# h1 split in rows and transposed by DMA in a two-layer graph attention kernel

## The chip, the cores and the metric

One core of one Trainium2 chip runs the whole program in one launch. The metric is the device time of an execution in microseconds; lower is better. Times of the profile count from the start of the profiled execution's span.

## The reference, cut to what matters

```python
x = _layernorm(x + gcn(x, W))                       # 1250 nodes, 768 features
h = gat_conv(x, W1, heads=4, out_ch=256)            # layer one: attention over the edges
h = relu(layer_norm(h, g1, be1))
h1 = h + (x @ Wr1 + br1)                            # 1250 x 1024
h = gat_conv(h1, W2, heads=1, out_ch=768)           # layer two; begins with h1 @ W2
h = layer_norm(h, g2, be2) + (h1 @ Wr2 + br2)
out = _layernorm(x + h)
```

In `gat_conv` each node sums the projected rows of its neighbours with softmax weights. Layer two needs two products of the same matrix, `h1 @ W2` and `h1 @ Wr2`.

## The kernel before, in words

The 1250 nodes are padded to 1280 and cut into T = 10 tiles of 128. Edges are counted into a dense 1280 x 1280 matrix, so that each attention is a dense matrix product. Every engine has its own hand-written list of instructions, in which it runs strictly in order; semaphores are the only ties between the lists. All DMAs that matter here are issued by SP (SyncE), one list as well: a wait in it holds up everything behind it.

Layer one's attention runs in 2 halves of the destination nodes (5 tiles each), each half in 4 heads, each head in 10 source tiles: 80 steps. In a step DVE makes the larger of two sums (L1576), ACT takes its exponential (L1163), DVE multiplies it by the edge counts (L1591), and PE multiplies the weights with the projected rows for 5 destination tiles (`attend1`, L972; float32, so each product shows as two instructions in the trace). DVE may be up to five steps ahead of PE (five weight buffers). `ATT_BANKS` (L99) gives each of the five sums of a head its PSUM bank: in the first half the heads walk over eight banks, in the second over six, since banks 6 and 7 hold `p_h`. When a head is done ACT evicts its five banks (`evict`), DVE makes the reciprocals (`sums`, L1564), ACT scales (`scale`).

A finished tile t of the attention, `att[t]` (128 nodes x 1024 features, float32), is normalized by DVE (`norm_start`, `norm_end`: L1406 to L1610), which also adds layer one's residual that SP loaded into `r_ld[t % 2]` (`residual`, L517). That is h1. Layer two's products need h1 with features on the partitions and in two float16 halves, high and low, since a product of halves is summed as high x high, high x low and low x high. Before the change a tile goes this way: PE transposes it by eight float32 128 x 128 transposes into `p_h`, two PSUM banks (`h1_transposes`, L960); ACT casts `p_h` to the high half (`h1_high`, L1139, in the helper L1060); DVE subtracts that from `p_h` for the low half (`h1_low`, L1615). There is one `p_h`, so the next tile's transposes wait for the low half of the one before.

Tiles 0 and 1 go this way inside the second half of the attention: DVE normalizes them at steps 9 and 18 (`NORM_AT`), PE transposes them after steps 11 and 20 (`TR_AT`), ACT and DVE split them at 15 and 26 (`H1_AT`). Tiles 2 to 9 follow behind the attention, where PE runs the list `LAYER2`: transposes `tr`, products with W2 `x` (48 matmuls each, `product2`, L945) and two products with Wr2 `r`; the other eight `r` come after it (L1019). Each product writes two adjoining banks, by turns one of two pairs (`p_x`), and waits in `slot_free` until the product two before it has been evicted. ACT and DVE meanwhile split W2 and Wr2 into halves (`weights(3)`, `weights(4)`, L1066 and L1257), whose rows SP loads two at a time, evict the products (`xl2_high`, `xl2_low`), and DVE normalizes the remaining tiles. On SP the loads of weights, residuals and of layer one's shift rows (`rows`) stand in one order, L519 to L552; `residual(t)` waits until tile t - 2 is normalized (L516), because the buffer is shared.

After the last `x` product, PE lays out a row of layer two's scores (`rows_of`, L986), DVE takes maxima, and the second attention (L1053) follows.

Earlier in the program SP already transposes something by DMA: ten transposes of 128 x 1280 two-byte elements (L462), in SBUF on both sides.

Of the kernel before, what the change touches and what calls it, by code (L numbers as in the profile page):

```python
# [74 lines left out]
C1 = 5  # L75
# [6 lines left out]
TR_AT = {11: 0, 20: 1}  # L82
H1_AT = {15: 0, 26: 1}
# [4 lines left out]
LAYER2 = ["tr2", "x0", "tr3", "x1", "x2", "tr4", "x3", "tr5", "x4", "tr6", "r0", "x5", "tr7", "r1", "tr8", "x6", "tr9", "x7", "x8", "x9"]  # L88
# [10 lines left out]
ATT_BANKS = [[(ch * C1 + j) % 8 for j in range(C1)] for ch in range(H)]  # L99
ATT_BANKS += [[(4 + ch * C1 + j) % 6 for j in range(C1)] for ch in range(H)]  # L100
# [8 lines left out]
def banks_read(ch, n):  # L109

    return ch * 2 * C1 + n
# [11 lines left out]
def gnn_program(nc, x, src, dst, W0, b0, W1, a_src1, a_dst1, b1, g1, be1, Wr1, br1,  # L123
# [7 lines left out]
    with ExitStack() as ctx:  # L131
# [152 lines left out]
        r_ld = [at(115 * KB, [HC], f32), at(119 * KB, [HC], f32)]  # L284
        h1t_hi = [at((b + 2 * j) * KB, [KH, P], f16) for b in (146, 95) for j in range(C1)]
# [56 lines left out]
        p_h = psum[:, 512 * 6:512 * 8]  # L342
# [12 lines left out]
        def everywhere(row):  # L355
# [13 lines left out]
            ln_var ln_rstd h1_ok h1_tr h1t_hi_ok h1t_lo_ok r_in0 r_in1   # L369
# [52 lines left out]
        PRODUCTS = [(step[0], int(step[-1])) for step in LAYER2 if step[0] != "t"] + [("r", t) for t in range(AHEAD_R, T)]  # L422
        X2_SLOT = [PRODUCTS.index(("x", t)) % 2 for t in range(T)]
        R2_SLOT = [PRODUCTS.index(("r", t)) % 2 for t in range(T)]
# [4 lines left out]
        def _(sp):  # L429
# [82 lines left out]

            def residual(t):

                if t >= 2:
                    sp.wait_ge(S["h1_ok"], t - 1)  # L516
                sp.dma_start(r_ld[t % 2], r1_d[t]).then_inc(S[f"r_in{t % 2}"], 16)  # L517
# [18 lines left out]
            rows(1, 2)  # L536
            weights(3, [2])
            rows(1, 3)
            residual(2)
            residual(3)  # L540
            weights(3, range(3, KH))
            sp.wait_ge(S["larger_ok"], 2 * H * T)
            weights(4, [0, 1])
            residual(4)
            weights(4, [2, 3])
            residual(5)
            residual(6)
# [145 lines left out]
        def _(pe):  # L693
# [260 lines left out]
            def h1_transposes(t):  # L954

                pe.wait_ge(S["h1_ok"], t + 1)
                if t:
                    pe.wait_ge(S["h1t_lo_ok"], t)
                for k in range(KH):
                    last = pe.transpose(p_h[:, k * P:(k + 1) * P], att[t][:, k * P:(k + 1) * P], ident)  # L960
                last.then_inc(S["h1_tr"], 1)
# [16 lines left out]
            for n in range(H * T):  # L978
                attend1(H * T + n)
                if n in TR_AT:  # L980
                    h1_transposes(TR_AT[n])
# [7 lines left out]
            def r2_first(t):  # L989

                product2(p_x[R2_SLOT[t]], t, W_PARTS[4], range(KH // 2))

            def r2_second(t):

                product2(p_x[R2_SLOT[t]], t, W_PARTS[4], range(KH // 2, KH)).then_inc(S["r2_done"], 1)

            def slot_free(i):

                if i < 2:
                    pe.wait_ge(S["att_read"], banks_read(2 * H - 1, C1 - 2 * (1 - i)))  # L1000
                else:
                    what, t = PRODUCTS[i - 2]
                    pe.wait_ge(S["xl2_lo_ok" if what == "x" else "r2_sb"], t + 1)
# [3 lines left out]
            for step in LAYER2:  # L1007
                t = int(step[-1])
                if step[:-1] == "tr":
                    h1_transposes(t)  # L1010
                else:
                    slot_free(PRODUCTS.index((step[0], t)))
                    if step[0] == "x":
                        xl2_tile(t)
                    else:
                        pe.wait_ge(S["w_lo"], W_FIRST[4] + KH)
                        r2_first(t)
                        r2_second(t)
# [39 lines left out]
        def _(act):  # L1058
# [74 lines left out]
            def xl2_high(t):  # L1133
                act.wait_ge(S["xl2_done"], t + 1)
                cast(xl2_hi[:, t, 0:D], p_x[X2_SLOT[t]][:, 0:D], S["xl2_hi_ok"], 1 / WSCALE)
# [34 lines left out]
            for n in range(H * T):  # L1170
                if n in W2_AT:
                    k = W2_AT.index(n)
                    act.wait_ge(S["p_free"], (H + 1 + (k > 2) + (k == KH - 1)) * T)
                    weights(3, [k])
                    if k == KH - 1:
                        act.wait_ge(S["w2a_split"], 2)
                        for m, part in enumerate((w2a_hi, w2a_lo)):
                            cast(w2_rows[:, :, m, D:XS], part[:, 0:KH - 1, :], S["w2x_ok"])
                            cast(w2_last[:, m, D:XS], part[:, KH - 1, :], S["w2x_ok"])
                if n in H1_AT:  # L1180
                    h1_high(H1_AT[n])
                exps(H * T + n)
# [3 lines left out]
            weights(4, [0, 1])  # L1186
            xl2_high(0)
            h1_high(3)
            weights(4, [2, 3])
            xl2_high(1)  # L1190
            weights(4, [4, 5])
            xl2_high(2)
            h1_high(4)
            weights(4, [6, 7])
            xl2_high(3)
            h1_high(5)
            xl2_high(4)
            h1_high(6)
            xl2_high(5)
            h1_high(7)  # L1200
# [47 lines left out]
        def _(dve):  # L1248
# [303 lines left out]
            def xl2_low(t):  # L1552

                p = p_x[X2_SLOT[t]]
# [72 lines left out]
            for n in range(H * T):  # L1627
                if n - 1 in W2_AT:
                    weights(3, [W2_AT.index(n - 1)])
                if n in H1_AT:  # L1630
                    h1_low(H1_AT[n])
# [12 lines left out]
            def r2_evict(t):  # L1644
# [4 lines left out]
                dve.scalar_tensor_tensor(to, p_x[R2_SLOT[t]][:, 0:D], 1 / WSCALE, xb, ALU.mult, ALU.add).then_inc(S["r2_sb"], 1)  # L1649
# [15 lines left out]
            norm_end(5)  # L1665
            weights(4, [4, 5])
            xl2_low(2)
            h1_low(4)
            norm_start(6)
            weights(4, [6, 7])  # L1670
            norm_end(6)
            xl2_low(3)
            h1_low(5)
# [7 lines left out]
            h1_low(6)  # L1681
            dve.wait_ge(S["dve"], steps_done())
            xb_sum(0)
            norm_start(8)
# [3 lines left out]
            h1_low(7)  # L1688
# [4 lines left out]
            h1_low(8)  # L1693
            xl2_low(6)
            h1_low(9)
# [150 lines left out]
```

## Time and profile before

| what | us |
|---|---|
| median of 3 runs | 851.09 |
| lowest and highest of them | 849.22, 853.28 |
| profiled execution, its own time | 851.03 |
| profiled execution, its span | 849.2 |

The span runs from the first to the last recorded instruction; 1.83 us of the execution lie around it. The profiled execution stands 0.06 us below the median. In the trace a row of a timeline has start, length, engine, line, operation, operands and count; in brackets is the idle time of the engine before it and what ended that. A merged row's length runs from its first start to its last end. The granted clock of TensorE is a fraction of 2.4 GHz.

### The profile page before, as it was taken

How to read it: one execution, taken by the hardware profiler on the slowest of the kernel's cores; microseconds unless marked ns; L12 is line 12 of the kernel's file. 1: busy time of each engine (PE TensorE's matmuls, PEld its weight loads, DVE VectorE, ACT ScalarE, POOL GpSimd, SP SyncE). 2: the span in 40 equal slices, each digit the busy share in tenths (PEclk: the TensorE clock that was granted, in tenths of full speed). 3: DMA queues.
4: the chain of work that ended last, by engine and by line, in shares of the span. 5: the costliest groups of instructions: out<-in, count | busy, mean ns of one | idle time of the engine just before them, and what ended most of it. 6: DMA issues, size and time to landing. Idle time of an engine off the chain costs nothing.

```text
span 849.2 us, 13556 instructions
## 1 busy us (share of the span) xinstructions
PE 818.0 (96%) x4922; PEld 526.0 (62%) x4922; DVE 670.3 (79%) x1181; ACT 270.3 (32%) x510; POOL 58.8 (7%) x77
## 2 busy tenths in 40 slices
PE   5999999999999999998999998999999999999995
PEld 4566666456454444436888887886666666655553
DVE  7998885778567849998888879969873196996686
ACT  3444444300111101014545545644301107760000
POOL 2000002000203000000000000002110000001111
PEclk9999999999999999999999999999999999999998
DMA  8000003114912474226111203213213242212232
GB/s 307 3 2 2 1 2 107 63 53 170 176 42 69 137 246 166 85 89 215 64 52 58 90 7 118 74 64 124 88 63 94 94 150 76 79 57 75 75 112 71
DMA packets 37709, 76.82 MB, mean 90 GB/s; under 512 B 15877, under 2 KB 16877, under 8 KB 37519
## 3 DMA queue, kind: packets, MB, share of 16 engines
q1 hardware_dynamic: 36382, 70.89, 25.3%
q0 software_dynamic: 1264, 5.11, 2.0%
q8 instruction: 38, 0.62, 0.3%
q14 instruction: 25, 0.20, 0.1%
HBM read 52.40 MB, written 20.31 MB: 86 GB/s over the span
## 4 chain that ended last, share of the span: by engine, by line
PE 80%; DVE 10%; DMA 3%; issue 3%; SPq 2%; DVEq 1%; ACT 1%; POOL 0%; POOLq 0%
PE psum L945 18%; PE psum L972 18%; PE psum L1053 12%; PE psum L868 8%; PE psum L747 8%; DVE arena L1445 6%; PE psum L759 6%; PE psum L811 4%; SPq L462 2%; PE psum L804 1%; PE psum L960 1%; PE psum L986 1%; DMA uv_scratch<-arena 1%; DMA arena<-as_scratch 1%; PE psum L720 1%
## 5 line engine op out<-in xcount | busy, mean ns | idle before, releaser
L972 PE MATMUL psum<-arena 128*128 128x257 f32 x800 | 175.4, 381 | 4.9 <-DVE arena L1591 3.8
L1060 ACT ACTIVATE arena<-psum 128x160 f16<-128x160 f32 (+6 forms) x188 | 93.3, 527 | 250.3 <-PE psum L747 73.9
L972 PEld LDWEIGHTS psum<-arena 128*128 128x128 f32 x800 | 151.2, 190 | 28.6 <-issue 2.7
L747 PE MATMUL psum<-arena 128*128 128x512 f16 x720 | 158.4, 379 | 2.3 <-DVE arena L1417 2.1
L945 PE MATMUL psum<-arena 128*128 128x512 f16 x960 | 158.5, 326 | 0.2 <-ACT arena L1060 0.2
L945 PEld LDWEIGHTS psum<-arena 128*128 128x128 f16 x960 | 93.5, 97 | 62.3 <-ACT arena L1060 0.5
L747 PEld LDWEIGHTS psum<-arena 128*128 128x128 f16 x720 | 69.5, 98 | 87.8 <-issue 7.0
L1053 PE MATMUL psum<-arena 128*128 128x512 f16 (+2 forms) x600 | 98.4, 325 | 0.0
L1445 DVE CUSTOM_DVE_ANT_0 arena<-arena 128x1280 bf16<-128x1280 bf16 x50 | 71.0, 1486 | 15.7 <-DMA arena<-as_scratch 9.8
L1053 PEld LDWEIGHTS psum<-arena 128*128 128x128 f16 x600 | 58.3, 97 | 39.8
L1163 ACT ACTIVATE arena<-arena 128x640 f32<-128x640 f32 x80 | 64.6, 835 | 52.8 <-DVE arena L1576 52.6
L1591 DVE SCALAR_TENSOR_TENSOR arena<-arena 128x640 f32<-128x640 f32 x80 | 65.2, 817 | 15.4 <-ACT arena L1163 9.6
L1060 ACT ACTIVATE arena<-arena 128x768 f16<-128x768 f32 (+4 forms) x58 | 45.7, 805 | 88.2 <-DMA arena<-in_L_gnn_Wr_dram 43.2
L1576 DVE SCALAR_TENSOR_TENSOR arena<-arena 128x640 f32<-128x640 f32 x80 | 70.0, 876 | 2.2 <-DMA arena<-uv_scratch 2.2
L868 PE MATMUL psum<-arena 128*128 128x512 f16 (+1 forms) x400 | 66.7, 326 | 2.7 <-DVE arena L1400 1.9
L759 PE MATMUL psum<-arena 128*128 128x512 f16 x360 | 68.5, 325 | 0.0
L868 PEld LDWEIGHTS psum<-arena 128*128 x400 | 38.3, 98 | 30.8 <-issue 6.2
L1359 DVE TENSOR_TENSOR arena<-arena 128x960 f16<-128x960 int16 x80 | 51.9, 649 | 0.0
L811 PE MATMUL psum<-arena 128*128 128x160 f16 x480 | 48.3, 235 | 1.6 <-DVE arena L1359 1.5
L1358 DVE TENSOR_TENSOR arena<-arena 128x768 f16<-128x768 int16 x80 | 44.2, 552 | 6.1 <-PE psum L811 2.4
L1455 DVE CUSTOM_DVE_ANT_0 arena<-psum,arena 128x256 bf16<-128x256 f32 x80 | 28.4, 420 | 19.8 <-PE psum L747 19.8
L759 PEld LDWEIGHTS psum<-arena 128*128 128x128 f16 x360 | 33.2, 97 | 15.5
(167 smaller groups left out, 695.5 us busy)
## 6 DMA issues: line engine op xcount, KB each, us to landing
arena<-in_L_gnn_W_dram SPq DMA_DIRECT2D x22, 384.0 KB, 3.6
r_scratch<-arena SPq DMA_DIRECT2D x10, 512.0 KB, 2.8
arena<-uv_scratch SPq DMA_DIRECT2D x16, 320.0 KB, 4.2
arena<-r_scratch SPq DMA_DIRECT2D x10, 512.0 KB, 3.7
x_scratch<-arena SPq DMA_DIRECT2D x10, 384.0 KB, 4.7
arena<-x_scratch SPq DMA_DIRECT2D x10, 384.0 KB, 3.5
r_scratch<-arena SPq DMA_DIRECT2D x10, 384.0 KB, 2.6
arena<-r_scratch SPq DMA_DIRECT2D x10, 384.0 KB, 4.0
```

What stands on the lines that cost most here:

```text
L747: ins = pe.matmul(o[:, a:b], part[:, k, ds(t * P, P)], w[:, k, a:b], start=(not begun and k == 0 and n == 0 and m == 0), stop=(k == kn - 1 ...
L759: last = pe.matmul(p_out[t % 2][:, a:b], part[:, k, t * P:(t + 1) * P], w[:, k, a:b], start=(k == 0 and name == "hh"), stop=(k == KD - 1 a ...
L811: last = pe.matmul(o, ring_lo[slot][:, i // 2, :, i % 2], ring_key[slot][:, i // 2, :, i % 2], start=False, stop=False, skip_group_check=True)
L868: ins = pe.matmul(p_out[par][:, a:b], counts, part[:, k, a:b], start=(not low and k == 0 and n == 0), stop=(not low and k == T - 1 and n = ...
L945: ins = pe.matmul(o[:, a:b], part[:, k, :], w[k][:, a:b], start=(k == 0 and n == 0 and m == 0), stop=(k == KH - 1 and n == 1))
L972: last = pe.matmul(p_att[:, ATT_BANKS[ch][j], 0:HID + 1], pf[n % PSLOTS][:, j * P:(j + 1) * P], xl[ch % H][:, k, 0:HID + 1], start=(k == 0 ...
L1053: last = pe.matmul(p_att2[c % 2][:, j, a:b], p[n][:, t % C1 * P:(t % C1 + 1) * P], xl2[:, k, a:b], start=(k == 0 and m == 0), stop=(k == T ...
L1060: act.activation(out_, in_, ACT.Copy, scale=scale).then_inc(signal, 1)
L1163: act.activation(ee[s], ee[s], ACT.Exp, bias=as_s[:, ch % H, k:k + 1]).then_inc(S["ex_ok"], 1)
L1445: dve.tensor_tensor_reduce(out=out_, in0=mask, in1=row, scale=1.0, scalar=NEG_BIG, op0=ALU.add, op1=ALU.max, accum_out=mx[:, col, t:t + 1] ...
L1576: dve.scalar_tensor_tensor(ee[s], u_row, asd[:, ch % H, k:k + 1], v_row, ALU.add, ALU.max).then_inc(S["larger_ok"], 1)
L1591: dve.scalar_tensor_tensor(pf[n % PSLOTS], ee[s], 1.0, CT[:, k, ds(ch // H * W1C, W1C)], ALU.min, ALU.mult).then_inc(S["pf_ok"], 1)
```

## The change

h1 is now split into halves before it is transposed. ACT casts `att[t]` as it lies, nodes on partitions, into a high half, DVE subtracts it for the low half, and SP sends each half through a DMA transpose of 128 x 1024 float16 into the same `h1t_hi[t]` and `h1t_lo[t]` as before. The halves (`h1_rows`) lie in the memory of the residual buffer `r_ld[t % 2]`, so `residual(t)` now waits until both transposes of tile t - 2 have landed. PE's transposes are gone, and with them `p_h`: the second half's attention banks walk over all eight, and layer two's products take turns over four bank pairs. The lists of SP, ACT and DVE are re-ordered to fit.

```diff
-TR_AT = {11: 0, 20: 1}
-H1_AT = {15: 0, 26: 1}
+HIGH_AT = {11: 0, 20: 1}
+LOW_AT = {12: 0, 22: 1}
-LAYER2 = ["tr2", "x0", "tr3", "x1", "x2", "tr4", "x3", "tr5", "x4", "tr6", "r0", "x5", "tr7", "r1", "tr8", "x6", "tr9", "x7", "x8", "x9"]
+LAYER2 = ["x0", "x1", "x2", "x3", "x4", "x5", "r0", "x6", "r1", "x7", "x8", "x9"]
-ATT_BANKS = [[(ch * C1 + j) % 8 for j in range(C1)] for ch in range(H)]
-ATT_BANKS += [[(4 + ch * C1 + j) % 6 for j in range(C1)] for ch in range(H)]
+ATT_BANKS = [[(ch * C1 + j) % 8 for j in range(C1)] for ch in range(2 * H)]
+        h1_rows = [[at((115 + 4 * i + 2 * m) * KB, [HC], f16) for i in range(2)] for m in range(2)]
-        p_h = psum[:, 512 * 6:512 * 8]
+        p_x2 = [psum[:, 1024 * i:1024 * (i + 1)] for i in range(4)]
+        SLOTS = [i % 4 for i in range(len(LAYER2))] + [1 + t % 2 for t in range(AHEAD_R, T)]
...
+            def h1_across(t):
+
+                for m, (made, to) in enumerate((("h1_hi_ok", h1t_hi[t]), ("h1_lo_ok", h1t_lo[t]))):
+                    sp.wait_ge(S[made], t + 1)
+                    sp.dma_start_transpose(to, h1_rows[m][t % 2]).then_inc(S[f"h1t_in{t % 2}"], 16)
+
             def residual(t):
 
                 if t >= 2:
-                    sp.wait_ge(S["h1_ok"], t - 1)
+                    sp.wait_ge(S[f"h1t_in{t % 2}"], 32 * (t // 2))
...
             rows(1, 2)
+            h1_across(0)
             weights(3, [2])
+            residual(2)
             rows(1, 3)
-            residual(2)
+            h1_across(1)
+            weights(3, [3])
             residual(3)
-            weights(3, range(3, KH))
+            weights(3, range(4, KH))
             sp.wait_ge(S["larger_ok"], 2 * H * T)
             weights(4, [0, 1])
+            h1_across(2)
             residual(4)
             weights(4, [2, 3])
+            h1_across(3)
             residual(5)
+            weights(4, [4, 5])
+            h1_across(4)
             residual(6)
-            weights(4, [4, 5])
+            weights(4, [6, 7])
+            h1_across(5)
             residual(7)
-            weights(4, [6, 7])
+            h1_across(6)
             residual(8)
-            residual(9)
...
+            h1_across(7)
+            residual(9)
             r2_store(0)
...
-            sp.wait_ge(S["h1_tr"], T)
+            h1_across(8)
+            h1_across(9)
...
             def xl2_tile(t):
 
-                pe.wait_ge(S["h1t_lo_ok"], t + 1)
-                product2(p_x[X2_SLOT[t]], t, W2_WIDE, range(KH), XS).then_inc(S["xl2_done"], 1)
+                pe.wait_ge(S[f"h1t_in{t % 2}"], 32 * (t // 2 + 1))
+                product2(p_x2[X2_SLOT[t]], t, W2_WIDE, range(KH), XS).then_inc(S["xl2_done"], 1)
...
                 if t == AHEAD_R:
                     pe.wait_ge(S["as2_ok"], 1)
+                    pe.wait_ge(S["xl2_lo_ok"], T)
+                    pe.wait_ge(S["r2_sb"], AHEAD_R)
...
             def h1_high(t):
-                act.wait_ge(S["h1_tr"], t + 1)
-                cast(h1t_hi[t], p_h.rearrange("p (k n) -> p k n", k=KH), S["h1t_hi_ok"])
+                act.wait_ge(S["h1_ok"], t + 1)
+                cast(h1_rows[0][t % 2], att[t], S["h1_hi_ok"])
...
             def h1_low(t):
 
-                dve.wait_ge(S["h1t_hi_ok"], t + 1)
-                dve.tensor_tensor(h1t_lo[t], p_h.rearrange("p (k n) -> p k n", k=KH), h1t_hi[t], ALU.subtract).then_inc(S["h1t_lo_ok"], 1)
+                dve.wait_ge(S["h1_hi_ok"], t + 1)
+                dve.tensor_tensor(h1_rows[1][t % 2], att[t], h1_rows[0][t % 2], ALU.subtract).then_inc(S["h1_lo_ok"], 1)
...
             sums(2 * H - 1)
+            h1_low(2)
             norm_start(3)
-            h1_low(2)
             norm_end(3)
             weights(4, [0, 1])
+            h1_low(3)
             norm_start(4)
             xl2_low(0)
-            h1_low(3)
             norm_end(4)
             weights(4, [2, 3])
+            h1_low(4)
             norm_start(5)
             xl2_low(1)
+            weights(4, [4, 5])
             norm_end(5)
-            weights(4, [4, 5])
+            h1_low(5)
```

The rest of DVE's list and ACT's list change in the same manner: each `h1_high(t)` and `h1_low(t)` now stands as soon as tile t is normalized.

## Rows read from the trace of the kernel before

**Rows 1.** The profile page, part 1: engine, busy us (share), instructions.

```profile
PE 818.0 (96%) x4922; PEld 526.0 (62%) x4922; DVE 670.3 (79%) x1181; ACT 270.3 (32%) x510; POOL 58.8 (7%) x77
```

**Rows 2.** Stretches: length, busy PE, PEld, DVE, ACT, POOL; clock, DMA share, GB/s.

```profile
500.00:521.00 21.00, 20.27 (x96) 17.37 (x96) 16.50 (x23) 10.85 (x20) 1.52 (x1) 1.00 0.23 76
...
580.00:600.00 20.00, 20.00 (x126) 12.16 (x125) 19.79 (x29) 7.10 (x9) 3.03 (x2) 1.00 0.56 183
```

**Rows 3.** Timeline of PE, attention's second half: start, us, line, [idle before <-releaser].

```profile
500.16 4.17 PE L972 MATMUL psum<-arena 128*128 128x257 f32 x18 [0.17 <-ACT arena L1060]
504.17 1.04 PE L960 MATMUL psum<-arena 128*128 128x128 f32 x8
...
521.99 2.87 PE L972 MATMUL psum<-arena 128*128 128x257 f32 x12 [1.55 <-DVE arena L1591]
525.57 2.00 PE L972 MATMUL psum<-arena 128*128 128x257 f32 x8 [0.72 <-ACT arena L1060]
...
548.56 21.51 PE L972 MATMUL psum<-arena 128*128 128x257 f32 x98 [0.17 <-ACT arena L1060]
569.90 1.04 PE L960 MATMUL psum<-arena 128*128 128x128 f32 x8
571.16 8.05 PE L945 MATMUL psum<-arena 128*128 128x512 f16 x48 [0.22 <-ACT arena L1060]
```

**Rows 4.** Line L960, TensorE's transposes: ns least/median/most.

```profile
L960 PE MATMUL psum<-arena x80: 272/272/273, 504.2 to 647.9; 128*128 128x128 f32 x80
```

**Rows 5.** Timeline of PE, layer two: the last transposition, then products.

```profile
647.13 1.04 PE L960 MATMUL psum<-arena 128*128 128x128 f32 x8
648.00 27.68 PE L945 MATMUL psum<-arena 128*128 128x512 f16 x168
```

**Rows 6.** Timelines of DVE, then ACT, around the attention's first transposition.

```profile
506.30 1.23 DVE L1615 TENSOR_TENSOR arena<-psum,arena 128x1024 f16<-128x1024 f32 x1 [3.44 <-ACT arena L1060]
...
505.24 1.02 ACT L1060 ACTIVATE arena<-psum 128x1024 f16<-128x1024 f32 x1 [3.32 <-PE psum L960]
```

**Rows 7.** Line L462, the ten DMA transposes: issue, then issue to landing.

```profile
L462 SPq DMA_TRANSPOSE arena<-arena x10: 1336/1606/3169, 216.1 to 232.8; - x10
...
DMA to landing us min/median/max: 3.6/4.4/6.2
```

**Rows 8.** Timeline of SP: the ten transposes, then weights beside the attention.

```profile
216.09 18.33 SPq L462 DMA_TRANSPOSE arena<-arena  x10
...
513.67 0.33 SPq L446 DMA_DIRECT2D arena<-in_L_gnn_W_dram  x1
...
525.94 23.91 SPq L446 DMA_DIRECT2D arena<-in_L_gnn_W_dram  x5
```

**Rows 9.** Lines L1615 and L1610 on DVE: ns least/median/most.

```profile
L1615 DVE TENSOR_TENSOR arena<-psum,arena x10: 1210/1217/1226, 506.3 to 649.3; 128x1024 f16<-128x1024 f32 x10
...
L1610 DVE SCALAR_TENSOR_TENSOR arena<-arena x10: 1224/1225/1226, 493.2 to 638.2; 128x1024 f32<-128x1024 f32 x10
```

**Rows 10.** ACT's groups by line and shape, 480 to 680 us.

```profile
L1060 ACT ACTIVATE arena<-arena 128x768 f16<-128x768 f32 x16 | 13.4, 844 | 9.1 <-DMA arena<-in_L_gnn_Wr_dram 8.8
...
L1060 ACT ACTIVATE arena<-psum 128x1024 f16<-128x1024 f32 x10 | 10.3, 1028 | 11.3 <-PE psum L960 11.0
```

**Rows 11.** Timeline of ACT, from 569 to 600 us.

```profile
570.18 2.40 ACT L1060 ACTIVATE arena<-psum 128x256 f32<-128x256 f32 x6
...
592.86 1.77 ACT L1060 ACTIVATE arena<-arena 128x768 f16<-128x768 f32 x2 [4.05 <-DMA arena<-in_L_gnn_Wr_dram]
```

**Rows 12.** Timeline of the SP queue beside layer two.

```profile
588.48 1.20 SPq L446 DMA_DIRECT2D arena<-in_L_gnn_Wr_dram  x2
```

**Rows 13.** Timeline of DVE: where two tiles' statistics start in layer two.

```profile
580.12 1.28 DVE L1406 BATCH_NORM_STATS2 arena<-arena 128x6 f32<-128x512 f32 x2
...
589.19 1.28 DVE L1406 BATCH_NORM_STATS2 arena<-arena 128x6 f32<-128x512 f32 x2
```

More of the change, by code:

```diff
@@ L368, in gnn_program @@
             uv_free uv_ok uv_tr uv_rows uv_dram uvr0 uvr1 ex_ok larger_ok pf_ok p_free rsum_ok att_read
-            ln_var ln_rstd h1_ok h1_tr h1t_hi_ok h1t_lo_ok r_in0 r_in1
+            ln_var ln_rstd h1_ok h1_hi_ok h1_lo_ok h1t_in0 h1t_in1 r_in0 r_in1
             w2a_in0 w2a_in1 w2a_ok w2a_split w2x_ok as2_ok as2_rows asr2
@@ L420, in gnn_program @@
                        [[w2[k][:, m, 0:D] for k in range(KH)] for m in range(2)], [wr2_hi, wr2_lo]]
-        PRODUCTS = [(step[0], int(step[-1])) for step in LAYER2 if step[0] != "t"] + [("r", t) for t in range(AHEAD_R, T)]
-        X2_SLOT = [PRODUCTS.index(("x", t)) % 2 for t in range(T)]
-        R2_SLOT = [PRODUCTS.index(("r", t)) % 2 for t in range(T)]
+        PRODUCTS = [(step[0], int(step[-1])) for step in LAYER2] + [("r", t) for t in range(AHEAD_R, T)]
+        SLOTS = [i % 4 for i in range(len(LAYER2))] + [1 + t % 2 for t in range(AHEAD_R, T)]
+        X2_SLOT = [SLOTS[PRODUCTS.index(("x", t))] for t in range(T)]
+        R2_SLOT = [SLOTS[PRODUCTS.index(("r", t))] for t in range(T)]
         UV2_AT = (5, 6)
@@ L949, in xl2_tile @@
             def xl2_tile(t):
-                pe.wait_ge(S["h1t_lo_ok"], t + 1)
-                product2(p_x[X2_SLOT[t]], t, W2_WIDE, range(KH), XS).then_inc(S["xl2_done"], 1)
[L954 to L961, printed above, removed]
+                pe.wait_ge(S[f"h1t_in{t % 2}"], 32 * (t // 2 + 1))
+                product2(p_x2[X2_SLOT[t]], t, W2_WIDE, range(KH), XS).then_inc(S["xl2_done"], 1)
             def attend1(n):
@@ L979, in _ @@
                 attend1(H * T + n)
-                if n in TR_AT:
-                    h1_transposes(TR_AT[n])
             def rows_of(column, tiles, o):
@@ L989, in r2_first @@
             def r2_first(t):
-                product2(p_x[R2_SLOT[t]], t, W_PARTS[4], range(KH // 2))
+                product2(p_x2[R2_SLOT[t]], t, W_PARTS[4], range(KH // 2))
             def r2_second(t):
-                product2(p_x[R2_SLOT[t]], t, W_PARTS[4], range(KH // 2, KH)).then_inc(S["r2_done"], 1)
+                product2(p_x2[R2_SLOT[t]], t, W_PARTS[4], range(KH // 2, KH)).then_inc(S["r2_done"], 1)
             def slot_free(i):
-                if i < 2:
-                    pe.wait_ge(S["att_read"], banks_read(2 * H - 1, C1 - 2 * (1 - i)))
-                else:
-                    what, t = PRODUCTS[i - 2]
-                    pe.wait_ge(S["xl2_lo_ok" if what == "x" else "r2_sb"], t + 1)
+                before = [n for n in range(i) if SLOTS[n] == SLOTS[i]]
+                if before:
+                    what, t = PRODUCTS[before[-1]]
+                    pe.wait_ge(S["xl2_lo_ok" if what == "x" else "r2_sb"], t + 1)
+                elif SLOTS[i] == 0:
+                    pe.wait_ge(S["att_read"], banks_read(2 * H - 2, C1 - 1))
+                else:
+                    pe.wait_ge(S["att_read"], banks_read(2 * H - 1, 2 * SLOTS[i] - 1))
             pe.wait_ge(S["w_lo"], W_FIRST[4])
@@ L1008, in _ @@
                 t = int(step[-1])
-                if step[:-1] == "tr":
-                    h1_transposes(t)
-                else:
[L1012 to L1018, printed above, removed]
+                slot_free(PRODUCTS.index((step[0], t)))
+                if step[0] == "x":
+                    xl2_tile(t)
+                else:
+                    pe.wait_ge(S["w_lo"], W_FIRST[4] + KH)
+                    r2_first(t)
+                    r2_second(t)
             for t in range(AHEAD_R, T):
@@ L1134, in xl2_high @@
                 act.wait_ge(S["xl2_done"], t + 1)
-                cast(xl2_hi[:, t, 0:D], p_x[X2_SLOT[t]][:, 0:D], S["xl2_hi_ok"], 1 / WSCALE)
+                cast(xl2_hi[:, t, 0:D], p_x2[X2_SLOT[t]][:, 0:D], S["xl2_hi_ok"], 1 / WSCALE)
             def h1_high(t):
-                act.wait_ge(S["h1_tr"], t + 1)
-                cast(h1t_hi[t], p_h.rearrange("p (k n) -> p k n", k=KH), S["h1t_hi_ok"])
+                act.wait_ge(S["h1_ok"], t + 1)
+                cast(h1_rows[0][t % 2], att[t], S["h1_hi_ok"])
             def evict(ch):
@@ L1179, in _ @@
                             cast(w2_last[:, m, D:XS], part[:, KH - 1, :], S["w2x_ok"])
-                if n in H1_AT:
-                    h1_high(H1_AT[n])
+                if n in HIGH_AT:
+                    h1_high(HIGH_AT[n])
                 exps(H * T + n)
@@ L1186, in _ @@
             weights(4, [0, 1])
+            h1_high(3)
             xl2_high(0)
-            h1_high(3)
             weights(4, [2, 3])
+            h1_high(4)
             xl2_high(1)
             weights(4, [4, 5])
+            h1_high(5)
             xl2_high(2)
-            h1_high(4)
             weights(4, [6, 7])
             xl2_high(3)
-            h1_high(5)
+            h1_high(6)
             xl2_high(4)
-            h1_high(6)
+            h1_high(7)
             xl2_high(5)
-            h1_high(7)
             h1_high(8)
@@ L1552, in xl2_low @@
             def xl2_low(t):
-                p = p_x[X2_SLOT[t]]
+                p = p_x2[X2_SLOT[t]]
                 dve.wait_ge(S["xl2_hi_ok"], t + 1)
@@ L1629, in _ @@
                     weights(3, [W2_AT.index(n - 1)])
-                if n in H1_AT:
-                    h1_low(H1_AT[n])
+                if n in LOW_AT:
+                    h1_low(LOW_AT[n])
                 if n in NORM_AT:
@@ L1648, in r2_evict @@
                 to, xb = (r_early, r_early) if t < AHEAD_R else (r2_st[t % 2], xb_ld[t % 2])
-                dve.scalar_tensor_tensor(to, p_x[R2_SLOT[t]][:, 0:D], 1 / WSCALE, xb, ALU.mult, ALU.add).then_inc(S["r2_sb"], 1)
+                dve.scalar_tensor_tensor(to, p_x2[R2_SLOT[t]][:, 0:D], 1 / WSCALE, xb, ALU.mult, ALU.add).then_inc(S["r2_sb"], 1)
             norm_start(2)
@@ L1653, in _ @@
             sums(2 * H - 1)
+            h1_low(2)
             norm_start(3)
-            h1_low(2)
             norm_end(3)
             weights(4, [0, 1])
+            h1_low(3)
             norm_start(4)
             xl2_low(0)
-            h1_low(3)
             norm_end(4)
             weights(4, [2, 3])
+            h1_low(4)
             norm_start(5)
             xl2_low(1)
+            weights(4, [4, 5])
             norm_end(5)
-            weights(4, [4, 5])
+            h1_low(5)
+            norm_start(6)
             xl2_low(2)
-            h1_low(4)
-            norm_start(6)
             weights(4, [6, 7])
             norm_end(6)
+            h1_low(6)
             xl2_low(3)
-            h1_low(5)
             dve.wait_ge(S["par_br2"], 16)
@@ L1680, in _ @@
             norm_end(7)
-            h1_low(6)
             dve.wait_ge(S["dve"], steps_done())
             xb_sum(0)
+            h1_low(7)
             norm_start(8)
@@ L1687, in _ @@
             xl2_low(5)
-            h1_low(7)
+            h1_low(8)
             norm_start(9)
@@ L1692, in _ @@
             r2_evict(1)
-            h1_low(8)
+            h1_low(9)
             xl2_low(6)
-            h1_low(9)
             xl2_low(7)
```

## The prediction

> **What bounds the kernel now.** I read the page first: PE is busy for 818.0 us of 849.2 [rows 1], so it matters what keeps PE busy and where it pauses. Next, the busy times by stretch: beside the attention PE works 20.27 of 21.0 us, and in layer two 20.00 of 20.0, while DVE there works 19.79 and the DMA engines 0.56 of their time for 183 GB/s [rows 2]. The granted clock is 1.00, the 2.4 GHz level, in both. So around the change PE is the bound, and DVE has almost nothing left in layer two. PE's timeline then shows the few pauses: 0.17, 1.55, 0.72 and 0.17 us in the attention's second half, 0.22 ahead of the first product [rows 3]. Everything that PE is spared here shortens the kernel, as long as nothing else comes late.
>
> **The transposes that go.** Eighty of them [rows 4], ten tiles of eight. One tile takes PE 0.87 us, from 647.13 to the next product at 648.00 [rows 5]. In the attention two stand in the row of work (504.17 [rows 3] is the first): 2 x 0.87 = 1.74 us. The third stands between the attention and the first product; from 569.90 to 571.16 are 1.26 us, the 0.22 us pause in it [rows 3]. The other seven: 6.09 us. Together **9.09 us**, all on PE's path.
>
> **The pauses in the attention.** The 1.55 us pause ends with a weight from DVE [rows 3]. DVE was late because it had itself stood 3.44 us before its low half of tile 0, waiting for ACT's cast, and ACT had stood 3.32 us for PE's transposes [rows 6]: ACT and DVE run ahead of PE and were made to wait for it. With the cast taken from `att[t]`, that circle is gone; the cast needs only DVE's own normalization. DVE gets back 3.44 us, PE needs its weights at most 1.55 + 0.87 + 0.17 = 2.59 us sooner, so 0.85 us are left and I count the pause as gone. The pauses of 0.17, 0.72 and 0.17 us are waits for ACT's evictions: with six banks, four of a head's five have been used by the head just before; with eight, only two, and PE comes to them after three other sums. I count them as gone: 0.17 + 1.55 + 0.72 + 0.17 = **2.61 us**.
>
> **The four bank pairs** are worth nothing by themselves: no product in layer two waits for its pair, and 168 matmuls from 648.00 run without a bracket in 27.68 us, or 7.9 us for a product's 48 [rows 5]. The new waits before the score row (all `xl2_low`, two `r2` evictions) stand behind work that DVE has ahead of `as2_ok`, which PE awaits there already. I take zero; the cover is DVE's order. The loads for the `r2` evictions, which stood behind PE's last transposes on SP, now stand behind the last DMA transposes; x8 and x9 cover them.
>
> **What is added: twenty DMA transposes on SP.** The row that comes nearest is the kernel's own ten, 128 x 1280 of the same two-byte kind: SP takes 1.34, 1.61, 3.17 us for one (least, median, most), and it lands 3.6, 4.4, 6.2 us after its issue [rows 7]. All ten go out in 18.33 us [rows 8]. Ours have eight blocks in place of ten. Those ten ran back to back, ours run between loads of residuals and weights; so I take the median, unscaled, as the likely cost, and keep both ends. The Trainium skill speaks against this part of the change (VectorE: DVE Perf Modes, The three transpose paths and Rules for kernel authors): a 128 x 128 transpose costs 390 ns on TensorE and 1309 ns through the DMA crossbar, and TensorE is the one to use where PSUM will do. A hundred blocks at that price would be 131 us, an estimate by that page; the trace disagrees with its 18.33 us [rows 8].
>
> The casts and subtractions only change their source. The subtraction from PSUM took 1.22 us, a DVE instruction on float32 from SBUF of the same size 1.225 us [rows 9]. ACT's cast from PSUM took 1.03 us; 768 elements from SBUF took 0.84, so 1024 between 1.03 and 1.13 us [rows 10]. Zero for both. ACT's cast of tile 0 now waits at step 11 for DVE, which has h1 ready at 493.2 + 1.2 = 494.4 [rows 9], eleven microseconds ahead of the old cast [rows 6]; behind it stand exponentials that DVE needs, but the cast was on ACT's list before too, so it adds nothing to the list, only shifts one cast four steps forward.
>
> **What is queued behind the new waits on SP.** In the attention `h1_across(0)` stands ahead of W2's third piece, which in the trace went out only at 513.67, and `h1_across(1)` ahead of the next, followed by pieces spaced over 23.91 us [rows 8]; the low halves of both tiles are due well before (steps 12 and 22), so the pieces lose at most the issue time, 2 x 1.61 us, on a queue that is waiting anyway. Zero, between 0 and 3 us of a DVE wait that PE has five weights against.
>
> In layer two it is tighter. PE would begin x0 at 571.16 - 1.74 - 1.26 - 2.61 = 565.55 us, and product x_t (t up to 5) is due at 565.55 + 7.87 t; x2 at 581.3, x5 at 604.9. ACT's cast of tile 2 stands behind the last eviction: together they end at 570.18 + 2.40 = 572.58, which is 2.68 us after the attention [rows 3, 11]; now 565.55 + 2.68 = 568.2. There `h1_across(2)` starts. SP's loop from tile to tile is two issues I, the landing D (residual t + 2 waits for it, and everything stands behind that), and some 1.5 us for a residual and two weights, 1.20 of it for the weights [rows 12]: L = 2I + D + 1.5. Tile 5 lands at 568.2 + 3L + 2I + D = 566.7 + 4L, so x5 is late by **4L - 38.2 us**. With the medians L = 3.22 + 4.4 + 1.5 = 9.1: early by 1.8. With the least values L = 7.8, early by 7. With the most L = 14.0, late by 18. A queue of loads ahead of the transposes can lengthen D: weights issued at 588.48 behind a residual released ACT at 592.86, 4.4 us on [rows 11, 12], no more than the transposes' own median. DVE has its own pace: from one tile's statistics to the next 580.12 to 589.19, 9.07 us [rows 13]. From the low half of tile 2 at 568.2 + 1.2 = 569.4, three such and one wait for ACT's cast (1.0) give 597.6 for the low half of tile 5, landed 1.6 + 4.4 later at 603.6; due 604.9. The margin is 1.3 us. After x5 stands r0, which needs no new tile, and after x6 stands r1, so later tiles have more. I put **0.7 us** of delay at x5, between 0 and 18.
>
> **The sum**, against the profiled execution's own 851.03 us (0.06 below the median of the runs, which is nothing): 851.03 - 9.09 - 2.61 + 0.7 = 840.03, so **840.0 us**.
>
> **The rivals.** First, layer two is paced by tiles, not by PE: L of 10 to 11.3, or a DVE pace of 10 us in place of 9.07. Then x5, and x3 and x4 before it, are late by 2 to 7 us: 841.3 to 846.3. For it: DVE is full there and the margin is 1.3 us. Against: both medians say otherwise. Second, DVE remains the bound in the attention, because 0.85 us of margin is little, and the 2.61 us stay: 842.6. Third, slower than before: the transposes, mixed with loads, cost what the dearest of the ten did. L = 14.0 and x5 starts 18 us late: 851.03 - 11.7 + 18 = 857.3. It decides from L = 13.5 on, where 4L - 38.2 exceeds 11.7 + 4.3. For it: the row's 3.17 and 6.2 us exist; against: each is one of ten, and issue and landing would have to be at their worst together. The Trainium skill's page named above (VectorE: DVE Perf Modes) points this way and further: sixteen blocks at 1309 ns are 20.9 us a tile, an estimate by that page, by which L would be 26.8 and the time 908; the ten transposes of the trace bear it out in nothing, and I give it no more than this rival's chance. Last, nothing changes: what PE is spared is waited for in full, x5 late by 11.7 us, L = 12.5: 851.
>
> **How the numbers follow.** The forecast (no delay to 2 us at x5) has 0.66, the first rival 0.16, the second 0.06, the third 0.06, no change 0.06. A measurement of this kernel can tell about 0.5% from no change, 4.3 us; faster means below 846.8. Forecast, second rival and nearly all of the first make 0.86, less a little for what I have not seen: 0.85. Same 0.08, slower 0.07. Range: low end 11.7 us off and the spread of runs below their median, 1.9: 851.03 - 11.7 - 1.9 = 837.4; high end within the first rival, 846.0. That leaves out about 0.19.
>
> **What would show it.** Right: no line of transposes on PE, no bracket over 0.2 us in the attention's second half, x0 at about 565.5, the score row at some 663 to 665, a DMA transpose of 1.2 to 1.7 us on SP. First rival: brackets on PE before x3 to x5 that end with a DMA. Second: a bracket near 520 that ends with DVE. Third: issues of 3 us and landings of 6. Wrong altogether if the transposes hold up the loads so that DVE or ACT wait for weights inside the attention.

## The result and the profile after

The changed kernel takes **836.85 us** (median of 4 runs, 835.29 to 837.94) against 850.74 us for the kernel before (4 runs): a ratio of 0.9832, 95% interval 0.9803 to 0.9862. The prediction said 840.0 us and 837.4 to 846.0: the direction was right, the gain of 13.9 us is larger than forecast, and the time lies 0.55 us below the low end of the range. The profiled execution takes 836.33 us, its span 834.5. One of the ten executions of the run that splits later, below, took 1220.27 us at a mean granted clock of 0.654 and is left out of its median.

The page, part 1, of the changed kernel, then its PE timeline from the attention to the second attention; these rows answer to [rows 1, 3, 5].

```profile
PE 807.4 (97%) x4842; PEld 517.7 (62%) x4842; DVE 670.2 (80%) x1181; ACT 269.2 (32%) x509; POOL 58.8 (7%) x77
```

```profile
389.13 173.65 PE L980 MATMUL psum<-arena 128*128 128x257 f32 x800 [0.98 <-DVE arena L1599]
562.62 98.39 PE L962 MATMUL psum<-arena 128*128 128x512 f16 x600
660.85 2.40 PE L992 MATMUL psum<-arena 128*128 128x128 f32 x20
...
726.04 9.23 PE L1061 MATMUL psum<-arena 128*128 128x512 f16 x55
```

PE is busy for 807.4 us, 10.6 less, and from the attention's first product on what is left runs without a bracket: 800 attention products in one row, right behind it layer two's 600 matmuls in one row up to the score row at 660.85. No line of transposes is left on PE. The stages, before and after, from their first rows:

| stage | before, us | after, us | gain, us |
|---|---|---|---|
| ahead of the attention | 390.67 | 389.13 | 1.54 |
| attention, with two of the ten transpositions | 179.23 | 173.49 | 5.74 |
| from the attention's end to the second attention | 170.82 | 163.42 | 7.40 |
| second attention, end, and what lies around the span | 110.31 | 110.29 | 0.02 |

The gain in the two stages that were changed is 5.74 + 7.40 = **13.14 us**. The busy times by stretch answer to [rows 2]:

```profile
500.00:521.00 21.00, 21.00 (x99) 18.38 (x98) 20.63 (x29) 13.01 (x24) 1.52 (x1) 1.00 0.29 88
580.00:600.00 20.00, 20.00 (x124) 11.85 (x122) 18.67 (x26) 7.58 (x9) 3.03 (x2) 1.00 0.81 184
```

PE works all the time in each stretch; DVE works 20.63 of 21.0 us in the first and 18.67 of 20.0 in the second; the share of the DMA engines in the second rose from 0.56 to 0.81 while they moved 184 GB/s in place of 183, the transposes' bytes included. The new transposes, line L518, answer to [rows 7]:

```profile
L518 SPq DMA_TRANSPOSE arena<-arena x20: 1232/1254/2742, 494.0 to 635.6; - x20
...
DMA to landing us min/median/max: 3.0/3.5/5.7
```

SP takes 1.25 us for one in the median, between the least and the median of the ten taken in proportion (0.8 x 1.34 = 1.07 us, 0.8 x 1.61 = 1.29 us), and it lands in 3.5 us.

### The profile page after: what moved, and what is told of

The parts are those of the page before. It is cut to its first block, busy times and chain, and to the rows that moved or that the text cites. A ratio compares the mean times of both kernels' runs of the same rounds, so it can differ in the third digit from the quotient of the medians.

```text
span 834.5 us, 13407 instructions
## 1 busy us (share of the span) xinstructions
PE 807.4 (97%) x4842; PEld 517.7 (62%) x4842; DVE 670.2 (80%) x1181; ACT 269.2 (32%) x509; POOL 58.8 (7%) x77
## 4 chain that ended last, share of the span: by engine, by line
PE 83%; DVE 9%; DMA 3%; SPq 2%; issue 2%; DVEq 1%; ACT 1%; POOL 0%; POOLq 0%
PE psum L980 21%; PE psum L962 19%; PE psum L1061 12%; PE psum L885 8%; PE psum L764 8%; DVE arena L1453 6%; PE psum L776 6%; PE psum L828 5%; SPq L463 2%; PE psum L821 1%; PE psum L737 1%; PE psum L992 1%; DMA arena<-as_scratch 1%; PE psum L839 1%; DMA arena<-uv_scratch 1%
## 5 line engine op out<-in xcount | busy, mean ns | idle before, releaser
L980 PE MATMUL psum<-arena 128*128 128x257 f32 x800 | 173.6, 380 | 1.0 <-DVE arena L1599 1.0
L1068 ACT ACTIVATE arena<-psum 128x160 f16<-128x160 f32 (+5 forms) x178 | 83.1, 498 | 206.7 <-PE psum L764 73.7
L962 PEld LDWEIGHTS psum<-arena 128*128 128x128 f16 x960 | 93.6, 97 | 62.8
L764 PEld LDWEIGHTS psum<-arena 128*128 128x128 f16 x720 | 69.5, 98 | 88.4 <-issue 7.6
L1068 ACT ACTIVATE arena<-arena 128x1024 f16<-128x1024 f32 (+3 forms) x68 | 56.2, 842 | 135.5 <-DVE arena L1618 47.7
L1061 PEld LDWEIGHTS psum<-arena 128*128 128x128 f16 x600 | 58.3, 97 | 39.8
L1103 ACT ACTIVATE arena<-psum 128x160 uint16<-128x160 f32 x80 | 24.4, 305 | 57.6 <-PE psum L776 36.7
```

The costliest lines, as they stand in the source:

```text
L764: ins = pe.matmul(o[:, a:b], part[:, k, ds(t * P, P)], w[:, k, a:b], start=(not begun and k == 0 and n == 0 and m == 0), stop=(k == kn - 1 ...
L962: ins = pe.matmul(o[:, a:b], part[:, k, :], w[k][:, a:b], start=(k == 0 and n == 0 and m == 0), stop=(k == KH - 1 and n == 1))
L980: last = pe.matmul(p_att[:, ATT_BANKS[ch][j], 0:HID + 1], pf[n % PSLOTS][:, j * P:(j + 1) * P], xl[ch % H][:, k, 0:HID + 1], start=(k == 0 ...
L1061: last = pe.matmul(p_att2[c % 2][:, j, a:b], p[n][:, t % C1 * P:(t % C1 + 1) * P], xl2[:, k, a:b], start=(k == 0 and m == 0), stop=(k == T ...
L1068: act.activation(out_, in_, ACT.Copy, scale=scale).then_inc(signal, 1)
```

## The experiments

**Six attention banks again.** The changed kernel; layer two's pairs in another order, so that x0 finds a free one.

```diff
-ATT_BANKS = [[(ch * C1 + j) % 8 for j in range(C1)] for ch in range(2 * H)]
+ATT_BANKS = [[(ch * C1 + j) % 8 for j in range(C1)] for ch in range(H)]
+ATT_BANKS += [[(4 + ch * C1 + j) % 6 for j in range(C1)] for ch in range(H)]
...
-        SLOTS = [i % 4 for i in range(len(LAYER2))] + ...
+        SLOTS = [(3, 1, 2, 0)[i % 4] for i in range(len(LAYER2))] + ...
...
```

> The changed kernel with the second half's attention sums on six banks again; everything else stays, the transposes on DMA too (layer two's products start on other pairs so that x0 need not wait). Before, the attention lost 4.0 us to pauses (179.23 us from its first product to its end, less 1.74 us of transposes, less 800 products at the 0.2169 us that one takes in the changed kernel). Theory: some 2.2 us of these are waits for ACT's evictions that six banks bring by themselves, the rest (1.55 us and the end of a product that the bracket does not count) is DVE. Then the attention takes 175.5 to 176 us here, against 173.5 in the changed kernel, and the time is about 839. Rival: ACT was late only because it had stood for PE's transposes; then six banks cost under 0.5 us and the time stays at 837.

Measured: 838.59 us, ratio 0.9862 (0.9827 to 0.9896). Its PE timeline:

```profile
388.89 109.33 PE L981 MATMUL psum<-arena 128*128 128x257 f32 x502 [1.29 <-DVE arena L1599]
498.39 21.94 PE L981 MATMUL psum<-arena 128*128 128x257 f32 x100 [0.17 <-ACT arena L1068]
520.51 21.94 PE L981 MATMUL psum<-arena 128*128 128x257 f32 x100 [0.17 <-ACT arena L1068]
542.62 21.51 PE L981 MATMUL psum<-arena 128*128 128x257 f32 x98 [0.17 <-ACT arena L1068]
563.97 36.25 PE L963 MATMUL psum<-arena 128*128 128x512 f16 x220
```

The attention takes 563.97 - 388.89 = 175.08 us, **1.59 us more** than the 173.49 us of the changed kernel. The theory holds; its size, 2.0 to 2.5 us, was too high. What readers should see: the brackets add up to 0.51 us, a third of what was lost.

**The kernel before, splitting later.**

```diff
-H1_AT = {15: 0, 26: 1}
+H1_AT = {18: 0, 27: 1}
```

> The kernel before with one line changed: ACT and DVE split tiles 0 and 1 at steps 18 and 27 of the attention's second half in place of 15 and 26; PE's transposes stay where they were. Theory: ACT stood 3.32 us for PE's transposes and DVE 3.44 us for ACT, and that made PE's 1.55 us pause near 522; asked three steps later, ACT finds the transposes done, both waits go, and PE's pause with them (1.55 us and the 0.16 us by which a product's length exceeds its share of the row): the attention takes 177.3 us or less from its first product to its end against 179.23, and the time is 848.5 to 849. Rival: DVE is late there by its own work (two normalizations in ten steps); then the bracket on PE that ends with DVE stays above 1 us and the time stays at 850.

Measured: 846.89 us (median of nine), ratio 0.9973 (0.9956 to 0.9990). The timelines of PE, then of ACT and of DVE at the first split:

```profile
388.72 109.33 PE L972 MATMUL psum<-arena 128*128 128x257 f32 x502 [1.25 <-DVE arena L1591]
498.22 4.17 PE L972 MATMUL psum<-arena 128*128 128x257 f32 x18 [0.17 <-ACT arena L1060]
...
503.10 17.94 PE L972 MATMUL psum<-arena 128*128 128x257 f32 x82
521.21 2.00 PE L972 MATMUL psum<-arena 128*128 128x257 f32 x8 [0.17 <-ACT arena L1060]
...
565.54 1.04 PE L960 MATMUL psum<-arena 128*128 128x128 f32 x8
```

```profile
503.30 1.02 ACT L1060 ACTIVATE arena<-psum 128x1024 f16<-128x1024 f32 x1 [0.45 <-PE psum L960]
```

```profile
507.08 1.22 DVE L1615 TENSOR_TENSOR arena<-psum,arena 128x1024 f16<-128x1024 f32 x1
```

ACT's cast waits 0.45 us where it waited 3.32, DVE's subtraction has no bracket where it had 3.44 [rows 6], and PE's bracket that ended with DVE is gone. So is most of the one of 0.72 us that ended with ACT: 0.17 is left. The attention takes 565.54 - 388.72 = 176.82 us, **2.41 us less** than before, with all of PE's transposes in place. The circle was the cause, and DVE's own work was not too much. What this attention still loses is 176.82 - 1.74 - 173.49 = 1.59 us, the same as with the six banks alone. So the two explain 2.41 + 1.59 = 4.00 us, all that the attention lost to pauses.

**PE's transposes put back as dead work.**

```diff
                 pe.wait_ge(S[f"h1t_in{t % 2}"], 32 * (t // 2 + 1))
+                for k in range(KH):
+                    pe.transpose(p_x2[X2_SLOT[t]][:, k * P:(k + 1) * P], ident, ident)
                 product2(p_x2[X2_SLOT[t]], t, W2_WIDE, range(KH), XS).then_inc(S["xl2_done"], 1)
```

> The changed kernel with eight float32 transposes of the identity put on PE before each of the ten x products; their results are overwritten and nothing waits for them. PE's work is then that of before, the waits are those of the changed kernel. Theory: PE's time is the path in all of layer two, so 10 x 0.87 = 8.7 us come back: 545.5 or so for 836.85 + 8.7 = 845.5. Rival: part of PE's spared time is waited for elsewhere (DVE's pace of 9 to 10 us a tile), then under 6 us come back, below 843.

(845.5 is meant where the text has 545.5.) Measured: 844.26 us, ratio 0.9924 (0.9898 to 0.9950). Its PE timeline:

```profile
564.90 1.04 PE L970 MATMUL psum<-arena 128*128 128x128 f32 x8
565.78 8.03 PE L962 MATMUL psum<-arena 128*128 128x512 f16 x48
...
609.51 15.84 PE L962 MATMUL psum<-arena 128*128 128x512 f16 x96
...
671.87 2.40 PE L994 MATMUL psum<-arena 128*128 128x128 f32 x20
```

From the attention's end at 564.90 to the score row at 671.87 are 106.97 us against 660.85 - 562.62 = 98.23: **8.74 us**, ten times the 0.87 us of one transposition [rows 5] within 0.04. PE's time is the path here, and nothing gives any of it back.

**Two bank pairs in layer two.**

```diff
-        SLOTS = [i % 4 for i in range(len(LAYER2))] + ...
+        SLOTS = [1 + i % 2 for i in range(len(LAYER2))] + ...
```

> The changed kernel with layer two's products on two bank pairs by turns in place of four (banks 2 to 5, as before the change). The prediction's step: the four pairs are worth nothing by themselves; then 0.6 us are lost before x0, which waits for the first eviction, and nothing later: about 837.5. Rival: in the changed order of DVE's list an eviction of a product comes two to five microseconds after the product two places on is due (the low half of x2 ends at 598.4, x4 is due at 594.1), so PE pauses before x3, x4, x6 and x7, in all 8 to 13 us: 845 to 850, most of the gain gone.

Measured: **853.61 us**, ratio 1.0044 (1.0026 to 1.0062): slower than the kernel before. PE's timeline, then two of the low halves on DVE:

```profile
564.02 23.78 PE L962 MATMUL psum<-arena 128*128 128x512 f16 x144 [0.74 <-ACT arena L1068]
588.64 8.05 PE L962 MATMUL psum<-arena 128*128 128x512 f16 x48 [0.83 <-DVE arena L1566]
598.93 23.72 PE L962 MATMUL psum<-arena 128*128 128x512 f16 x144 [2.25 <-DVE arena L1566]
627.09 18.39 PE L962 MATMUL psum<-arena 128*128 128x512 f16 x96 [4.44 <-DVE arena L1566]
648.60 29.36 PE L962 MATMUL psum<-arena 128*128 128x512 f16 x168 [3.12 <-DVE arena L1566]
677.80 2.40 PE L992 MATMUL psum<-arena 128*128 128x128 f32 x20
```

```profile
597.92 0.95 DVE L1566 SCALAR_TENSOR_TENSOR arena<-psum,arena 128x768 f16<-128x768 f32 x1
...
626.08 0.95 DVE L1566 SCALAR_TENSOR_TENSOR arena<-psum,arena 128x768 f16<-128x768 f32 x1
```

PE starts x4 at 598.93, when DVE's low half of x2 ends (597.92 + 0.95), and x6 at 627.09, when that of x5 ends (626.08 + 0.95). The rival holds in its mechanism, and its size, 845 to 850, was too small: the brackets add up to 11.38 us, but the stage, from the attention's end (it starts at 389.64, and 389.64 + 173.49 = 563.13) to 677.80, takes 16.44 us more than 98.23. Some 0.8 is the length of a product in front of each bracket. The rest is in the matmuls: 96 of them from 627.09 take 18.39 us, where e3's 96 took 15.84. The busy times by stretch say why:

```profile
598.90:622.60 23.70, 23.67 (x144) 13.94 (x144) 18.10 (x24) 3.74 (x4) 3.03 (x2) 1.00 0.51 109
627.00:633.00 6.00, 5.91 (x21) 2.90 (x22) 5.60 (x9) 0.19 (x1) 1.51 (x1) 0.56 0.73 150
633.00:639.00 6.00, 6.00 (x38) 3.53 (x37) 1.79 (x2) 1.28 (x2) 1.13 (x2) 1.00 0.41 124
648.60:654.00 5.40, 5.40 (x23) 2.82 (x24) 0.00 (x0) 0.00 (x0) 0.00 (x0) 0.68 0.94 241
```

The third figure from the end of a row, behind POOL's, is the granted clock: 1.00 between the pauses of 2.25 and 4.44 us, a mean of 0.56 for the 6 us after the one of 4.44 us, then 1.00 again, and 0.68 for 5.4 us after the one of 3.12.

**Three bank pairs.**

```diff
-        SLOTS = [i % 4 for i in range(len(LAYER2))] + ...
+        SLOTS = [i % 3 for i in range(len(LAYER2))] + ...
```

> The changed kernel with layer two's products on three bank pairs by turns. With two pairs PE paused 11.4 us for DVE's low halves of the products two places back (the longest, 4.44 us, before x6). Theory: a third pair gives each eviction one product more, 7.9 us, which is longer than the longest pause, so none is left, and the time is that of the changed kernel, 837. Rival: DVE's lateness grows as PE no longer waits for it (9 to 10 us a tile against PE's 7.9), then pauses of 1 to 4 us are left before x5 or x7 and the time is 838 to 841.

Measured: 837.98 us, ratio 0.9845 (0.9824 to 0.9865). Its PE timeline:

```profile
565.13 98.40 PE L962 MATMUL psum<-arena 128*128 128x512 f16 x600
663.37 2.40 PE L992 MATMUL psum<-arena 128*128 128x128 f32 x20
```

No bracket; 663.37 - 565.13 = 98.24 us. The theory holds: the third pair is what counts, the fourth is spare.

**Twice the DMA transposes.**

```diff
...
                     sp.dma_start_transpose(to, h1_rows[m][t % 2]).then_inc(S[f"h1t_in{t % 2}"], 16)
+                    if 2 <= t < 8:
+                        sp.wait_ge(S["p_free"], 2 * H * T)
+                        sp.dma_start_transpose(spare[m], h1_rows[m][t % 2]).then_inc(S[f"h1t_in{t % 2}"], 16)
...
```

> The changed kernel in which each half of tiles 2 to 7 goes through a second DMA transpose into spare memory, counted on the same semaphore. A pair was issued in 2.61 us and landed some 4.7 us later in the stage with loads. By the prediction's loop, SP takes 4 x 1.3 + 4.7 + 1.5 = 11.4 us a tile from 565.3 on, tile 5 lands at 565.3 + 3 x 11.4 + 5.2 + 4.7 = 609.4, x5 was due at 602.0: 7.4 us late, PE pauses before x3, x4 and x5 that end with a DMA, about 844. Rival: DVE and ACT set the pace of the tiles (SP waited 45.9 us for ACT in this stage) and the transposes fit between; then under 2 us.

Measured: 842.53 us, ratio 0.9908 (0.9873 to 0.9942). PE's timeline, then where SP begins tiles 3, 4 and 5:

```profile
564.28 31.65 PE L970 MATMUL psum<-arena 128*128 128x512 f16 x192
597.02 8.04 PE L970 MATMUL psum<-arena 128*128 128x512 f16 x48 [1.08 <-DMA arena<-arena]
607.66 59.03 PE L970 MATMUL psum<-arena 128*128 128x512 f16 x360 [2.61 <-DMA arena<-arena]
666.53 2.40 PE L1000 MATMUL psum<-arena 128*128 128x128 f32 x20
```

```profile
576.41 1.24 SPq L523 DMA_TRANSPOSE arena<-arena  x1
...
586.93 1.24 SPq L523 DMA_TRANSPOSE arena<-arena  x1
...
598.23 1.24 SPq L523 DMA_TRANSPOSE arena<-arena  x1
```

The stage takes 666.53 - 564.28 = 102.25 us, 4.02 more, and the pauses stand before x4 and x5 and end with a DMA. Neither expectation has the size: the transposes do delay the tiles, as the theory says, but at half the price, since a tile takes 598.23 - 586.93 = 11.3 us here only once; the two loops ahead of it took 9.4 and 10.5. The theory's 11.4 us counted one issue twice, as the prediction's loop did (x5, below); without it the loop is 3 x 1.3 + 4.7 + 1.5 = 10.1 us.

**The changed kernel once more.**

> The changed kernel once more, unaltered, for the size of its gain. In the two profiles it was 14.70 us, of which 1.54 us lie ahead of the attention, where nothing was changed (its start was 389.13 against 390.67 us; in four other kernels it lay between 388.9 and 391.4). Theory: that share is chance, and the gain is the 13.1 us that the stages from the attention on show: a median of 837 to 838 against 850.3. Rival: the change also sets something ahead of the attention; then the attention starts near 389.1 again and the gain is 14 us or more.

Measured: 837.02 us against 850.24 us for the kernel before in the same series, 13.2 us less; ratio 0.9838 (0.9823 to 0.9854). The ratio's interval alone would allow the rival's 14 us; the start decides: the attention starts at 390.17, not near 389.1, and the stages behind it are those of the first profile:

```profile
390.17 173.64 PE L980 MATMUL psum<-arena 128*128 128x257 f32 x800 [1.62 <-DVE arena L1599]
...
661.88 2.40 PE L992 MATMUL psum<-arena 128*128 128x128 f32 x20
```

The start of the attention lay at 388.72 to 391.65 us in the nine profiles, of kernels that are alike up to there. The 1.54 us ahead of it are chance; the 13.14 us are the change. This is also why the experiments are compared by their stages: with the dead transposes and with twice the DMA transposes the medians lie 7.41 and 5.68 us above the changed kernel's 836.85, where the stages give 8.74 and 4.02.

## Why the prediction was wrong

**The path and the transposes: right.** PE was the bound, and the 9.09 us came: 7.40 behind the attention, where the step had 1.26 + 6.09 = 7.35, and 1.74 in it. The runs show the latter too: the attention that splits later has two transpositions, the one on six banks has none, both have the same three brackets of 0.17 us for ACT, and 176.82 - 175.08 is 1.74.

**The pauses in the attention: the step that failed, in its size.** "I count them as gone: 0.17 + 1.55 + 0.72 + 0.17 = 2.61 us." They are gone, but they were worth **4.00 us**: 179.23 us less 1.74 of transposes leave 177.49, and the 800 products take 173.49 when nothing stops them. The mechanism was right part by part (2.41 for the circle of ACT, DVE and PE, 1.59 for the banks). The reading was not. A bracket is the idle time after the end of the instruction before it, and a product is shown with 0.38 us while one starts every 0.217; so each bracket lacks 0.16 us, and a shorter pause has no bracket at all. By the single starts in the trace, the product after the first one behind each of the four brackets is late too, by 0.10 us, and one more wait for ACT, before a product at 478.48, costs 0.28 us and shows no bracket: 2.61 + 4 x 0.26 + 0.28 = 3.93 of the 4.00 us. The counts of products in the same 22 us of the kernel before and of the changed one, line `attend1` alone, show it in a view:

```profile
478.00:500.00 22.00, 21.98 (x101) 18.59 (x99) 1.00 0.11 31
```

```profile
478.00:500.00 22.00, 22.00 (x104) 19.26 (x103) 1.00 0.21 55
```

Before, PE is busy for 21.98 of 22.00 us and yet has 101 instructions where the changed kernel has 104: three times 0.217 us that the busy time hides. The starts say the same: the first 502 products reach from 390.67 to 500.16 [rows 3], 109.49 us, where 502 at the pitch of the changed kernel, 173.49 / 800 = 0.2169 us, take 108.87; 0.62 us are lost, and the one bracket there shows 0.17.

**x5 late by 0.7 us: wrong, it is not late.** The formula 4L - 38.2 rested on L = 2I + D + 1.5, which adds to the landing the issue that the landing already holds. SP's timeline of the changed kernel:

```profile
593.38 4.03 SPq L518 DMA_TRANSPOSE arena<-arena  x2
599.50 0.33 SPq L524 DMA_DIRECT2D arena<-r_scratch  x1
603.68 2.62 SPq L518 DMA_TRANSPOSE arena<-arena  x2
```

The two transposes of tile 5 are issued from 593.38 to 597.41, for 1.24 and 2.74 us; the next residual goes out when the second has landed, at 599.50. The second landed in 4.8 us: counted from its issue's start at about 594.7 that gives 599.5, counted from its end it would be 602.2. So L = I + D + 1.5, shorter by one issue, and tile 5 lands 2.5 us before x5 starts at 562.62 + 5 x 7.87 = 601.97. The step's bound by DVE counted the same issue twice ("landed 1.6 + 4.4 later"): without it its margin of 1.3 us is 2.9, and 2.5 came. SP was not the pace anyway:

```profile
SPq L518 <- ACT arena L1068: 45.9, 7, 14.3
...
SPq L524 <- DMA arena<-arena: 13.0, 7, 2.1
```

From 480 to 690 us it waited 45.9 us for ACT's casts and 13.0 for its own transposes. The casts wait for DVE's normalization, so the pace is DVE's, as the other bound of that step said:

```profile
575.16 1.28 DVE L1414 BATCH_NORM_STATS2 arena<-arena 128x6 f32<-128x512 f32 x2
...
584.24 1.28 DVE L1414 BATCH_NORM_STATS2 arena<-arena 128x6 f32<-128x512 f32 x2
...
593.39 1.23 DVE L1623 TENSOR_TENSOR arena<-arena 128x1024 f16<-128x1024 f32 x1 [1.12 <-ACT arena L1068]
...
597.42 0.95 DVE L1566 SCALAR_TENSOR_TENSOR arena<-psum,arena 128x768 f16<-128x768 f32 x1
```

One tile's statistics to the next are 9.08 us here [rows 13 had 9.07], and the low half of tile 5 starts at 593.39, after the wait for ACT's cast that the step allowed for. That is 30.77 us after the attention's end, where the step had 597.6 - 1.2 - 565.55 = 30.85. Tiles 0 and 1, ready before x0, are lead enough for this up to r0. From tile 5 on SP takes over 10 us a tile (593.38 to 603.68), the pace of the first rival, but there r0 and r1 stand between the x products, and no bracket follows.

**The four bank pairs "are worth nothing by themselves": wrong.** The step took the trace of before, where no product but x0 (0.22 us, for ACT) waited for its pair, as the cover. That cover was DVE's order together with PE's transposes, as DVE's row for the low half of x2 in the kernel before shows:

```profile
597.20 0.94 DVE L1558 SCALAR_TENSOR_TENSOR arena<-psum,arena 128x768 f16<-128x768 f32 x1
```

It ends at 598.14, and with four transpositions between the attention's end and it x4 started only at 605.29. In the changed order the low half of x2 ends at 597.42 + 0.95 = 598.4 and x4 is due at 594.1. Counted from the attention's end, x4 is 3.9 us earlier than before (31.5 in place of 35.4) and the low half 7.5 us later (35.8 in place of 28.2): DVE's new order took more of the cover than the missing transposes did; no run parts the two. Two pairs cost 16.4 us there, more than the change gains. The sum was not touched by this, as the change has four pairs; had the step been followed in a design, it would have lost everything.

**The sum and the range.** The sum lies 840.03 - 836.33 = 3.70 us above the profiled execution: 1.39 of it are the pauses, 0.70 x5, 0.05 the transposes and 0.02 the end; 1.54 us lie ahead of the attention and are chance. The signs by position missed for the same reasons: x0 came at 562.62 and not at 565.5, which is 1.39 + 1.54 us. The range's low end was the sum without delay less the runs' spread, 837.4; with 4.00 us in place of 2.61 it would have been 836.0. Without the 1.54 us of chance the change comes to 851.03 - 13.14 = 837.89, just inside: that the time fell out of the range is in part bad luck, that the pauses were priced too low is not.

**The rivals.** None came about in the time. DVE had lead enough in the attention; the transposes did not cost what the dearest of the ten did (a most of 2.74 and 5.7 us, once each). The price of the Trainium skill (VectorE: DVE Perf Modes, The three transpose paths), 1309 ns for a block of 128 x 128 through the DMA crossbar, does not hold for blocks sent together: here a DMA of eight was issued in 1.25 us and landed in 3.5.

## What to carry to other kernels

Price a pause on a pipelined engine by counting its instructions in a stretch against the count of an undisturbed one, not by adding up idle brackets: here the brackets showed 2.61 of 4.00 us. When a step is taken off the engine that bounds, work that ran ahead of it and was made to wait for it is freed too, and moving the wait by three steps gave 2.4 us without any of the rest. And when the bound gets faster or another engine's list is re-ordered, look at every buffer that was deep enough: two bank pairs did before, three do now.

## What was not expected of the hardware

After a pause of 4.44 us on PE the granted clock was 0.56 on average over the next 6 us, after one of 3.12 us it was 0.68 over 5.4 us, means between the levels of 2.4 and 1.2 GHz, while after one of 2.25 us it stayed at 1.00 (two bank pairs, above), and also after one of 2.61 (twice the DMA transposes). It cost 2.5 us for 96 matmuls and 1.7 us for 168 (29.36 us against 27.68 [rows 5]). Twelve microseconds of waiting (11.38 and some 0.8) came to sixteen that way.

Sixteen of the twenty DMA transposes, 256 KB each, ran between ordinary loads on one queue, and the loads landed as before: in the median 4.2 us for a piece of Wr2 (4.3 before), 3.9 for a residual (3.7 before). The 184 GB/s from 580 to 600 us, against 183 before, contain four transposes, 52 GB/s; the same total took 0.81 of the DMA engines' time in place of 0.56.
